# Attention weights with keys on partitions: scores computed twice in place of transposes, attends in runs of four

## The reference

```python
q = (Q @ Wq.T + bq).reshape(bs, n, H, HD).transpose(0, 2, 1, 3)      # Q = layernorm(x)
k = (K @ Wk.T + bk).reshape(bs, n, H, HD).transpose(0, 2, 1, 3)      # K = V = context
scores = jnp.einsum('bhqd,bhkd->bhqk', q, k) / math.sqrt(HD)
scores = jnp.where(causal[None, None], scores, -jnp.inf)
probs = jax.nn.softmax(scores, axis=-1)
out = jnp.einsum('bhqk,bhkd->bhqd', probs, v)
x = x + jnp.tanh(gate) * (out.transpose(0, 2, 1, 3).reshape(bs, n, D) @ Wo.T + bo)
```

## Time and profile before

| | us |
|---|---|
| median of three timed executions | 1894.08 |
| lowest, highest | 1890.63, 1894.83 |
| profiled execution: span from its first to its last instruction | 1942.7 |
| TensorE busy in it | 1620.1 (83%) |
| VectorE, ScalarE, POOL busy | 1242.5, 1210.7, 740.3 |
| stage L1, from its first to its last scores | 697.9 to 952.0 |
| end of L1's last output product | 960.7 |
| stage L3, from its first to its last scores | 1420.6 to 1715.9 |
| end of the last routing step in L3 | 1739.9 |

### The profile page before, as it was taken

One profiled execution on the slowest core, in us unless ns is written; L12 is line 12 of the kernel. 1 busy time (PEld: TensorE's weight loads), 2 busy tenths in 40 slices (PEclk: granted clock), 3 DMA queues, 4 the chain that ended last, 5 costly groups with the idle time before them and its releaser, 6 DMA issues. The chain is left out here.

```text
span 1942.7 us, 38924 instructions
## 1 busy us (share of the span) xinstructions
PE 1620.1 (83%) x12739; PEld 1206.0 (62%) x12739; DVE 1242.5 (64%) x3348; ACT 1210.7 (62%) x4192; POOL 740.3 (38%) x712
## 2 busy tenths in 40 slices
PE   4399999599999769999789966999579887866994
PEld 3355554379999546666589855545456555644994
DVE  5599999488888666767567755213457656654444
ACT  2189999189999557877667742433168656631444
POOL 2145555245555542111067835002222332333542
PEclk9799999699999889999889987999689888977997
DMA  3320000110000042423191022100044433313224
GB/s 127 74 106 1 1 1 1 34 45 2 1 2 2 28 116 76 105 72 89 32 320 54 1 88 86 42 0 1 19 121 114 124 101 84 88 55 97 70 70 156
DMA packets 63845, 126.40 MB, mean 65 GB/s; under 512 B 10670, under 2 KB 27233, under 8 KB 61529
## 3 DMA queue, kind: packets, MB, share of 16 engines
q1 hardware_dynamic: 53658, 103.10, 18.6%
q10 hardware_dynamic: 5616, 12.06, 1.9%
q0 software_dynamic: 4384, 8.89, 1.3%
HBM read 91.00 MB, written 50.43 MB: 73 GB/s over the span
## 5 line engine op out<-in xcount | busy, mean ns | idle before, releaser
L1531 ACT ACTIVATE L_E<-L_sc,L_negm 128x128 f32<-128x128 f32 x1024 | 300.1, 402 | 153.2 <-DVE L_negm L1399 152.5
L593 ACT ACTIVATE B_E<-B_logits,B_m 128x32 f32<-128x32 f32 (+1 forms) x1792 | 365.2, 374 | 8.8 <-DVE B_m L562 7.9
L599 POOL TENSOR_TENSOR B_E<-B_E,B_r 128x512 f32<-128x512 f32 x256 | 268.0, 1047 | 264.5 <-DVE B_r L581 264.5
L1399 DVE TENSOR_REDUCE L_negm<-L_sc 128x4 f32<-128x512 f32 x256 | 174.9, 686 | 87.0 <-PE L_sc L1640 74.9
L562 DVE TENSOR_REDUCE B_m<-B_logits 128x16 f32<-128x512 f32 (+1 forms) x256 | 172.8, 675 | 38.4 <-PE B_logits L553 31.2
L1638 PE MATMUL L_sc<-KS,L_QS 128*128 128x512 f32 x256 | 143.8, 562 | 54.5 <-DMA L_QS<-L_qsplit 37.1
L576 DVE TENSOR_REDUCE B_r<-B_E 128x16 f32<-128x512 f32 (+1 forms) x256 | 172.9, 675 | 2.5 <-POOL B_E L599 1.3
L1539 ACT ACTIVATE L_PT<-L_pt 128x512 f32<-128x512 f32 x256 | 165.9, 649 | 6.3 <-DMA picked_rows<-A_ys 6.0
L1648 PE MATMUL L_pt<-ident,L_E 128*128 128x128 f32 x1024 | 160.1, 280 | 0.8 <-ACT L_PT L1539 0.8
L551 PE MATMUL B_logits<-B_phihi,B_xhi 128*128 128x512 f32 x256 | 153.5, 600 | 5.1 <-DVE B_philo L538 2.5
L1648 PEld LDWEIGHTS L_pt<-ident,L_E 128*128 128x128 f32 x1024 | 126.6, 145 | 23.9 <-issue 2.5
(11 more groups left out here) (348 smaller groups left out, 3598.5 us busy)
## 6 DMA issues: line engine op xcount, KB each, us to landing
route_rows<-in_F_fill SPq DMA_DIRECT2D x33, 516.0 KB, 19.7
KS<-L_ksplit SPq DMA_DIRECT2D x180, 64.0 KB
L_QS<-L_qsplit SPq DMA_DIRECT2D x42, 256.0 KB
F_xg<-route_rows SPq DMA_DIRECT2D x71, 64.5 KB
ew<-in_expert_w SPq DMA_DIRECT2D x1, 4096.0 KB, 15.4
L_cT<-in_ctxT SPq DMA_DIRECT2D x16, 256.0 KB
L_qsplit<-L_qhi ACTq DMA_DIRECT2D x16, 256.0 KB, 2.7
L_qsplit<-L_qlo ACTq DMA_DIRECT2D x16, 256.0 KB, 5.8
```

Source lines behind the costliest of these rows:

```text
L593: ins = nc.scalar.activation(e[:, cols], self.bank(k)[:, cols], ACT.Exp, bias=self.m[:, k % 4, g:g + 1])
L599: self.st.nc.gpsimd.tensor_tensor(e, e, self.r[:, k % 2, :].unsqueeze(2) .to_broadcast([128, self.ng, self.size]), ALU.mult).then_inc(self ...
L1399: nc.vector.tensor_reduce(negm[:, k % 4, :], sc[k % 2][:].rearrange("p (h k) -> p h k", h=NHG), AX.X, ALU.max, negate=True).then_inc(s["ma ...
L1531: ins = nc.scalar.activation(e[:, h * 128:(h + 1) * 128], sc[k % 2][:, h * 128:(h + 1) * 128], ACT.Exp, bias=negm[:, k % 4, h:h + 1])
```

## The change

The weights are not transposed. The scores of a unit are computed a second time, eight slots (LAG) later, with the keys as weights and the queries as moving columns, so that keys stand on partitions; the exponential of that (one activation of 512 columns, without bias) is at once the operand of `attend`. The shift must then be part of the product: the maxima of the plain scores, split in two parts (`widen`, VectorE), are transposed once per sequence (`turn_shifts`), and copied by ScalarE to partitions 96 to 127 of QS (`shift_rows`), while KS holds a pattern there that picks the right row for each head. So plain scores use 96 partitions, turned ones 128. Units and shifts take the two banks `sT` by turns (`place_of`).

Attends run for four units in a row. The order is by slots t = 0 to END; uses have new slots; v is computed in slot 11 and taken in slot 13, x is moved by ScalarE, not VectorE; without `rope` the high parts come straight from the bank (ScalarE) and the low parts by VectorE, not POOL. The router's products come in slots 38, 41 and 50 after their group's first slot, its scatters one to a slot.

```diff
+    PUT = {"k": -6, "kr": -5, "x": -4, "q": -2, "qr": -1, "v": 11}
+    PUT_SECOND = {"k": 0, "kr": 1, "x": 2, "q": 4, "qr": 5, "v": 11}
+    OUT = 30
+    ROWS, LOGITS, RANKS = 38, 41, 50
+    LAG, TURN, ATTEND, DIVIDE, RP = 8, 6, 14, 16, 8
...
+    def slot(use, m):
+        if use == "out":
+            return UG * m + OUT
+        if use in ("rows", "logits", "ranks"):
+            return UG * m + {"rows": ROWS, "logits": LOGITS, "ranks": RANKS}[use]
+        return (PUT_SECOND if m == 1 else PUT)[use] + UG * (m - 1)
...
+    for t in range(END):
+        if t >= TURN and (t - TURN) % NHG == 0 and (t - TURN) // NHG < B:
+            place_of["rows", (t - TURN) // NHG] = len(place_of)
+        if 0 <= t - LAG < NU:
+            place_of["unit", t - LAG] = len(place_of)
...
 @block.sync
+            for i, way in enumerate(("mask", "maskT")):
+                sp.dma_start(mi[:, i, :], d[f"{name}_{way}"]).then_inc(s["w_in"], 16)
+            if first:
+                sp.dma_start(pick[:], d["pick"]).then_inc(s["w_in"], 16)
...
+                    put_keys(n)
+                    if n >= 2:
+                        sp.wait_ge(s["sT_ready"], place_of["unit", (n - 1) * UG - 1] + 1)
+                    spread_keys(n)
...
 @block.vector
+            def widen(b):
+                w = wide[b % 2]
...
+                nc.vector.tensor_copy(w[:, 96:112], negm[b % 2][:]).then_inc(s["wide_set"], 1)
+                v.wait_ge(s["wide_set"], b + 1)
+                nc.vector.tensor_tensor(w[:, 112:128], negm[b % 2][:], w[:, 96:112].bitcast(F32), ALU.subtract)\
+                    .then_inc(s["wide_ready"], 1)
...
+            for t in range(END):
...
+                if due:
+                    invert(b)
...
+                    for use in uses:
+                        if use != "x" and t == slot(use, m) + (1 if rope and use != "v" else 2):
+                            take(use, m)
...
+                if t < NU:
+                    maximum(t)
+                    if t % NHG == NHG - 1:
+                        widen(t // NHG)
+                if due:
+                    divide(b)
...
 @block.scalar
+            def exponent(k):
+                i = place_of["unit", k]
+                a.wait_ge(s["sT_ready"], i + 1)
+                if k >= RP:
+                    a.wait_ge(s["av_done"], k - RP + 1)
+                nc.scalar.activation(PT[k % RP][:], sT[i % 2][:], ACT.Exp).then_inc(s["sT_used"], 1)
+            def shift_rows(b):
+                i, n, j = place_of["rows", b], b // GB, b % GB
+                a.wait_ge(s["sT_ready"], i + 1)
+                nc.scalar.activation(QS[n % 2][96:128, :, j * 128:(j + 1) * 128],
+                                     sT[i % 2][96:128, 0:128].unsqueeze(1).to_broadcast([32, NHG, 128]), ACT.Copy)\
+                    .then_inc(s["sT_used"], 1)
...
+            if first:
+                a.wait_ge(s["w_in"], 16 * NW)
+                for u in range(2):
+                    nc.scalar.activation(p.KS[u][96:128, :, :, :].rearrange("p g h k -> p (g h) k"),
+                                         pick[96:128, :].unsqueeze(2).to_broadcast([32, NHG * NHG, GD]), ACT.Copy)\
+                        .then_inc(s["picks_set"], 1)
...
 @block.tensor
+            def turn_shifts(b):
+                i = place_of["rows", b]
+                t_.wait_ge(s["wide_ready"], b + 1)
+                if i >= 2:
+                    t_.wait_ge(s["sT_used"], i - 1)
+                nc.tensor.transpose(sT[i % 2][:, 0:128], wide[b % 2][:].bitcast(F32), p.ident[:]).then_inc(s["sT_ready"], 1)
+            def mask_of(at, way, begins):
+                return nc.tensor.matmul(at, p.ident16[:], mneg[:, way:way + 1, :].to_broadcast([128, NHG, 128]),
+                                        start=begins, stop=not begins, skip_group_check=True)
+            def turned(k, c):
                 n, j, hg = k // UG, k // NHG % GB, k % NHG
+                return nc.tensor.matmul(sT[place_of["unit", k] % 2][:, c * 128:(c + 1) * 128],
+                                        p.KS[n % 2][:, hg, c, j * 128:(j + 1) * 128], QS[n % 2][:, hg, j * 128:(j + 1) * 128],
+                                        start=False, stop=True, skip_group_check=True)
+            def scores(k, kT):
+                plain, other = k < NU, 0 <= kT < NU
...
+                if other:
+                    i = place_of["unit", kT]
+                    t_.wait_ge(s["sT_used"], max(i - 1, place_of["rows", kT // NHG] + 1))
...
+                    mask_of(sT[i % 2][:], 1, True)
+                    turned(kT, 0)
+                if plain:
...
+                    if k >= 2:
+                        t_.wait_ge(s["max_ready"], k - 1)
+                    nc.tensor.matmul(sc[k % 2][:], QS[n % 2][0:96, hg, j * 128:(j + 1) * 128],
+                                     p.KS[n % 2][0:96, hg, :, j * 128:(j + 1) * 128], start=True, stop=False,
+                                     skip_group_check=True)
+                if other:
+                    turned(kT, 1)
+                if plain:
+                    mask_of(sc[k % 2][:], 0, False).then_inc(s["sc_ready"], 1)
+                if other:
+                    turned(kT, 2)
+                    turned(kT, 3).then_inc(s["sT_ready"], 1)
...
+            for t in range(END):
+                if t >= TURN and (t - TURN) % NHG == 0 and (t - TURN) // NHG < B:
+                    turn_shifts((t - TURN) // NHG)
+                scores(t, t - LAG)
+                for use, m in puts.get(t, ()):
...
+                if t >= ATTEND and (t - ATTEND) % NHG == 0 and t - ATTEND < NU:
+                    for k in range(t - ATTEND, t - ATTEND + NHG):
+                        attend(k)
```

More of the change, by code:

```diff
@@ L1113, in stage_attn @@
     uses = ["k", "kr", "x", "q", "qr", "v"] if rope else ["k", "x", "q", "v"]
[L1114 to L1120, removed]
+    PUT = {"k": -6, "kr": -5, "x": -4, "q": -2, "qr": -1, "v": 11}
[3 more added lines that the diff above has]
+    LAG, TURN, ATTEND, DIVIDE, RP = 8, 6, 14, 16, 8
     NU = NG * UG
+    ROUTED = range(NG - 1) if route else ()
+    END = NU + (RANKS - 2 * UG + 6 if route else OUT - UG + 6)
     FIRST = [use for use in uses if not (keyed and use == "k")]
+    def slot(use, m):
[4 more added lines that the diff above has]
+        return (PUT_SECOND if m == 1 else PUT)[use] + UG * (m - 1)
+    puts = {}
+    for m in range(NG):
+        for use in (uses if m else []) + ["out"] + (["rows", "logits", "ranks"] if m in ROUTED else []):
+            puts.setdefault(slot(use, m), []).append((use, m))
     turn_of = {}
@@ L1126, in stage_attn @@
             turn_of[use, 0] = len(turn_of)
[L1127 to L1141, removed]
+    for t in range(END):
+        for put in puts.get(t, ()):
+            turn_of[put] = len(turn_of)
+    place_of = {}
+    for t in range(END):
[3 more added lines that the diff above has]
+            place_of["unit", t - LAG] = len(place_of)
     with Stage(nc, name) as st:
@@ L1176, in stage_attn @@
         sc = [st.bank(f"sc{i}") for i in range(2)]
-        pt = [st.bank(f"pt{i}") for i in range(2)]
+        sT = [st.bank(f"sT{i}") for i in range(2)]
         pp = [st.bank(f"pp{i}") for i in range(2)]
@@ L1363, in take @@
                 bank = aux[a % 2]
[L1364 to L1367 removed]
+                if use == "v":
+                    v.wait_ge(s["aux_full"], a + 1)
                     if n >= 2:
@@ L1454, in route_part, with route_parts @@
                     v.sem_inc(route.slot_ready, 1)
+            def route_parts(t, half):
+                for m in ROUTED:
+                    i, j = (2 * (t - slot(use, m) - 1) + half for use in ("logits", "ranks"))
+                    if 0 <= i < route.PICKS:
+                        route_part(m, i)
+                    if 0 <= j < route.PARTS - route.PICKS:
+                        route_part(m, route.PICKS + j)
             c = turn_of["const", 0]
```

451 lines of the change are left out of this document (200 added, 251 removed).

## The result

| | median us | lowest to highest | executions |
|---|---|---|---|
| before | 1893.09 | 1890.63 to 1894.83 | 4 |
| changed | 1972.12 | 1969.96 to 1987.61 | 4 |

**The change costs 79 us: ratio 1.042, interval 1.037 to 1.047.** The direction is as forecast, the size is not (1909, at most 1950). The profiled execution of the changed kernel took 1971.9 us, its span is 1970.1.

What follows compares the result with a forecast made beforehand. L1 was taken as bound by TensorE (93%), L3 as also losing time to a router bubble. L1 +26.9 and L3 -12.0 gave +14.9 on the median 1894.1: 1909 us, range 1868 to 1950.

Steps and rivals of the forecast that it cites:

- The difference I put on the median unscaled: Whole kernel: +14.9 us, worked out on a profile spanning 1942.7, added to the timed median 1894.1, giving 1909.
- step 8: L3: TensorE's pause around the router in late groups goes, 282.7 us against 295.3; drain +1.1, start -0.5: -12.0 together.
- 1. TensorE's work: Per unit: transposes out (0.43 us), second mask and four turned products in; slot 1.04 against 1.00, work does not fall.
- Rival B: Turned products cost 0.107 us each: +13.4 and +1.0 in L1, +10.4 in L3, 1934 us; 17%.
- 2. Runs of four: Attends: entering and leaving costs 0.2 us, shared by four units instead of two, saving 0.05 a unit.
- (a): Two banks sT shared by units and turned shifts: TensorE loses 0.8 to 0.9 us four times a group, +3.3.
- (b): x in slot 12 needs the bank of v, which VectorE takes only in slot 13: TensorE sits 1.8 us.
- (c): Plain scores wait for the maximum of two slots before, from VectorE's heavy slots: 0.9 us a group.
- 6. Start: Start of L1: ScalarE's two pick pattern writes, 14.1 us, precede the first k; with added loads +7.7 us.
- 7. L1's drain and L3's start: Turned scores come eight slots late: L1's end takes 15.0 us against 8.7, +6.3; L3's start -0.5.
- Rival C: L3's late-group pause stays, caused by the scatters and not ScalarE: 5 x 6 us more, 1939; 12%.
- rival A: TensorE never waits, groups cost their work: 1840 us, or 1875 with half the waits gone; 27%.

Runs made afterwards that it cites:

- second profile: The kernel before, unchanged, profiled once more: it took 1894.49 us, with a span of 1892.4.

## Why the prediction was wrong

**The sum's base failed first.** It is the step "The difference I put on the median unscaled", with step 8's bubble in it. It took the 48.6 us by which the span stood over the median for something that both kernels carry. It sat in one execution, and mostly in one stage of it. Between the first profile of before and the profile after, the difference is 27.4 and the forecast was 14.9; the other 50.3 us are the distance between the two profiles of before (1942.7 to 1892.4), 38.4 of them in L3, 5.1 in L1 and 7.0 in L3's drain. The signs were in the rows: L3's first three groups at about 31, the full ones behind them at 41, with a clock of 0.52. With the 256.8 of the second profile for L3, the same sum, 26.9 in L1 and 282.7 less 256.8 in L3, would have said about 1947; with 248.9 for L1 too, 1952.

**By its steps:**

1. TensorE's work: right. A plain slot is 1.04 as worked out, and TensorE's busy time in L1 rises by 9.2, 6.5 of it the clock's. Rival B (0.107 for each of the four) fell with the same slot: a bare product does take 0.10, but four of them put together lengthened the slot by 0.05 alone.
2. Runs of four: the saving (0.05) is right in size. The step costed only that and not what the bunching does to those who feed TensorE. Alone it costs 51 us in the kernel before, and 14 against pairs in the changed one.
3. ScalarE: 100.1 us of 278.4 in L1, or 12 of 32; near the 14 foreseen, and as foreseen without use.
4. Waits: (a) 30 waits in L1, slots of 1.89 against 1.04, 0.85 each as foreseen; in idle time 16.5. (b) 1.9 at five of six x and 1.7 at one, foreseen 1.8. (c) 4.4 in L1, 6.3 foreseen; in L3 9.6. The groups without low clock are 35.8 to 36.8, 36.2 foreseen. **The term that is missing is what the clock does behind such pauses**: the forecast looked for lower clock in L3 only, and expected it gone; no term of its sum prices it. It is 6.5 us more than before in L1 and 7.3 in L3. L1 was foreseen at 267.0 and is 278.4: 6.8 in two groups of 39.6, 2.9 in the first group (29.8 for 26.9), 1.7 in the others.
5. Q's waits inside L1 went from 6.9 us, by the second profile, to 1.1.
6. Start: 7.7 foreseen, 7.4 against the profile I had, 8.9 against the second; ScalarE's two writes took 13.94 for 14.1.
7. L1's drain and L3's start: +5.8 foreseen, +5.5 against the first profile and +3.0 against the second.
8. L3: 282.7 foreseen, 280.0 measured, but with the wrong parts: groups of 37 to 39 come from the waits and the clock, not from pauses without a cause. The bubble that was to go was not there. The drain, foreseen at +1.1, is +12.5 (+5.5 against the first profile). In the second profile of before the router's last logits come 6 us behind the last scores, the output 7.5, the ranks 15.5; after, eight slots of turned products and the late attends stand in front, and they come 14, 20 and 24 us behind. The first product of the next stage, in the second profile of before:

```profile
1692.97 1.12 PE L1049 MATMUL F_h<-ident,R_XR 128*128 128x128 f32 x4 [3.91 <-DVE R_XR L1025]
```

and in the changed kernel:

```profile
1757.89 1.16 PE L1661 MATMUL L_aux<-L_W,L_OT 128*128 128x128 f32 x8 [1.38 <-DVE L_OT L1438]
1761.88 0.19 PE L1061 MATMUL L_aux<-R_M,R_strict 128*128 128x32 bf16 x1 [2.83 <-DVEq L1469]
1770.06 1.12 PE L1049 MATMUL F_h<-ident,R_XR 128*128 128x128 f32 x4 [7.91 <-DVE R_XR L1025]
```

I had walked L1's drain (+6.3) and given L3's a sixth of that, though the router's chain lies in it. Why the drain grew is read from the two orders; no run changes the drain alone.

**Rival C** (L3's bubble stays) and **rival A** (TensorE never waits) fell: in the second profile of before there was no bubble, and every wait was there. Of the 63 us between 1909 and 1972 the base is then 50; the other 12.5 are L1, 11.4 over its sum, and L3's drain, 4.4 over, less 2.7 in L3 and two small terms. The direction was right for L1's reasons alone: L3 was to gain 12 us and lost about as much as L1. That a separate bank for the turned shifts would end the bank wait without moving it wasn't tried: all eight PSUM banks are in use, and the free columns lie in the banks of the attends, which TensorE would write while ScalarE read there.

## What to carry to other kernels

Before a sum is made on a profile, compare its span with the timed median; if they differ by more than the effect, find the rows that hold the difference (equal groups of unequal length, a low granted clock) and use the ordinary ones. Where the bounding engine was 95% busy (L1 before), relieving the second engine was worth next to nothing, and the evenness of what the bounding engine was fed was worth more than a saving in its own instructions: bunching that was to save 0.05 us a unit cost 51 us. Price a pause of the bounding engine with the low clock that can follow, and judge such edits together, since each alone leaves a pause that gives its gain back.

## What was not expected of the hardware

Pauses of TensorE of 1.3 to 1.9 us in an otherwise busy stretch were in part followed by 3.4 or 6.8 us at the lower clock, worth 1.7 or 3.4 us each. The same pause had this behind it in two of six groups of L1, and with x's pause shortened to 0.9 in none. The same L3 code, but for where the pick pattern is written, lost 11.3, 20.1 and 22.9 us to the clock in three kernels that differ in L1. That is enough to hide an edit of 8 us that the trace shows plainly at its own place.
